# A decoder layer on one core: means and variances of the linear attention from rounded sums and their remainders, with roundings on ScalarE

## The chip, the core and the metric

The kernel runs on one core of a Trainium2 chip. The core has five engines that each work through their own instructions in order: TensorE (PE, with its weight loads as PEld), VectorE (DVE), ScalarE (ACT), GpSimd (POOL) and SyncE (SP, which only issues DMAs here). They wait for each other through semaphores. The metric is the device time of one execution in microseconds (us), the median of several.

## What is computed

A decoder layer over 8 batches of 512 tokens with 256 features. It has three parts, each followed by a layer norm. The first, linear attention within chunks of 32 tokens, is the one that the change is about:

```
Q, K, V = x @ W_q.T, x @ W_k.T, x @ W_v.T
S = (Qc @ Kc.T) * mask              # per chunk of 32 tokens, mask = decay ** (i - j) for i >= j
O = S @ Vc
out = sigmoid(x @ W_g.T) * O @ W_o.T + x
x = layernorm(x + out)
```

Then come a cross attention with 16 heads (`x = layernorm(x + xattn(x, ctx))`) and a feed-forward part with ternary weights and a low-rank term, of which only the weights concern us:

```
h = bitlinear(x, w_fc) + gate * (x @ v.T @ fast_b.T @ u.T)
out = bitlinear(relu(h) ** 2, w_proj)
```

## The kernel before

All activations are held with features on the 128 partitions (two halves, `DK` = 2) and the 512 tokens of a batch along the free dimension. The three parts are three phases. Each engine's program of a phase is one function (`_(pe)`, `_(dve)`, `_(act)`, `_(pool)`, `_(sp)`), written in the order in which it runs; nothing is reordered by a scheduler, and semaphores join the engines.

Where precision allows no plain rounding, an operand is split in two fp32r tiles, the rounded value (`_hi`) and the remainder (`_lo`), and three products hi·hi, lo·hi and hi·lo replace one fp32 product (`split_matmul`, L48 to L50). Plain fp32 products are kept for the scores (L57), attend (L747), the mean (L715), the variance (L719), and for some weight work.

The linear-attention phase goes through the batches in steps. Step b (1 to 7) works on batch b and finishes batch b - 1 and b - 2. In the order of each engine:

- TensorE (`step`, L770): `gates(b)` (12 products), `variance(b-2)`, `queries(b)` (12), `outputs(b-1)` (12), `scores(b)`, `values(b)` for tiles 0 and 1, `mean(b-1)`, `values(b)` for tiles 2 and 3, `attend(b)`. After step 2 comes `scale_means`, after steps 3 and 4 `low_rank`, whose result enters the feed-forward weights.
- VectorE (`step`, L631): `finish_y(b-1)` (two y_a, then tile_sum), `root(b-2)`, `mask_scores(b)`, `scale_x1(b-2)` (tile x_a), `split_x(b+1)` (x_hi, x_lo), `subtract_mean(b-1)` (dev_a), `gated(b)` (og_a), `sum_squares(b-1)`, `split_gated(b)` (og_hi, og_lo), and some weight work at the end.
- ScalarE (a loop at L480): `front(b)` (gate, with two table loads), `query_copies(b)` (qm), `deviation(b-2)` (three operations for the inverse root), `values(b)` (copies to v_tok), `square(b-1)` (sq_a).
- SyncE (`load_and_store`, L370): the load of x for batch b + 1 waits until y of batch b - 1 is finished (`y_out`), since it goes in the same half of `x_in`; behind it comes the store of x1.
- GpSimd splits the weights wq, wk and wv of the next phase (L405, L407), each after a load of 1 MB, and later works on the ternary weights (L414 to L423).

`tile_sum` holds first y's sum over the two halves, for the mean, and then the sum of the squares, for the variance. Both go through a product with `mean_w`, a 128x128 matrix of 1/256, into the PSUM bank `ST`.

The last batch's parts (`variance_late`, `outputs_last`, `mean_last`, `variance_last`) are issued by the cross-attention phase, among its first keys, queries and values. The cross attention and the feed-forward phase are not touched.

## Time and profile before

| | us |
|---|---|
| median of 3 runs | 1280.46 |
| lowest and highest | 1279.95, 1281.04 |
| the profiled execution | 1279.73 |
| its span, first to last instruction | 1277.7 |
| TensorE busy | 1256.6 (98%) |
| VectorE busy | 922.2 (72%) |
| ScalarE busy | 794.0 (62%) |
| GpSimd busy | 768.3 (60%) |

An engine's busy time is the time in which it has an instruction under way. Matmuls overlap in their pipeline, so a record is longer than what it takes from the stream; what a product costs is read from the distance of the starts. An fp32 product leaves two records, an fp32r product one. The chain of waits follows the end of the run back, at each step to what released it.

### The profile page before, as it was taken

What the parts mean: (1) busy time and instruction counts of PE and PEld (TensorE: products, weight loads), DVE (VectorE), ACT (ScalarE), POOL (GpSimd) and SP (SyncE); (2) the same over time, 40 slices, a digit from 0 to 9 for tenths busy, and PEclk for the clock granted to TensorE, in tenths of its full rate; (3) what the DMA queues carried; (4) which work ended last, traced back from release to release, by engine and by line L of the source; (5) the groups of instructions that cost most, each with busy time, mean ns of one, the idle gap of its engine ahead of it and who ended that gap; (6) DMA issues with size and microseconds to landing.
All of it is one profiled execution on the core that took longest, in us unless ns stands there. A gap on an engine that the chain in (4) does not pass through costs nothing.

```text
span 1277.7 us, 21198 instructions
## 1 busy us (share of the span) xinstructions
PE 1256.6 (98%) x6900; PEld 844.6 (66%) x6900; DVE 922.2 (72%) x1816; ACT 794.0 (62%) x1061; POOL 768.3 (60%) x445
## 2 busy tenths in 40 slices
PE   8999999999999999999999999999999999999996
PEld 6887856666666666656665666657566655677775
DVE  6888877656775767477577756784766777778887
ACT  3444457655665656566656655574656676788885
POOL 2532368967876679487768767794877687100000
PEclk9999999999999999999999999999999999999999
DMA  6311220001100110010011001100200110021101
GB/s 221 116 67 50 69 66 18 4 1 34 37 2 17 33 19 0 17 50 2 0 33 35 0 17 33 19 0 17 50 2 0 34 18 17 14 70 50 49 17 50
DMA packets 99391, 43.08 MB, mean 34 GB/s; under 512 B 77168, under 2 KB 82048, under 8 KB 99344
## 3 DMA queue, kind: packets, MB, share of 16 engines
q1 hardware_dynamic: 98528, 39.33, 12.4%
q0 software_dynamic: 816, 3.15, 0.7%
q8 instruction: 27, 0.44, 0.1%
q14 instruction: 20, 0.16, 0.0%
HBM read 29.59 MB, written 12.58 MB: 33 GB/s over the span
## 4 chain that ended last, share of the span: by engine, by line
PE 92%; DVE 3%; POOL 2%; issue 1%; ACT 1%; DMA 1%; SPq 0%; POOLq 0%; DVEq 0%
PE ps L1400 17%; PE ps L1375 15%; PE ps L48 12%; PE ps L50 11%; PE ps L49 11%; PE ps L1391 4%; PE ps L1379 4%; PE ps L1436 2%; PE ps L1435 2%; PE ps L1437 2%; PE ps L1412 2%; PE ps L1829 2%; PE ps L1830 2%; PE ps L747 1%; PE ps L57 1%
## 5 line engine op out<-in xcount | busy, mean ns | idle before, releaser
L1200 DVE CUSTOM_DVE_ANT_0 junk<-ps,mask 128x512 bf16<-128x512 f32 x504 | 315.0, 687 | 87.7 <-PE ps L1391 86.3
L1066 ACT ACTIVATE prob<-ps,mcol 128x1024 f32<-128x1024 f32 x256 | 282.2, 1117 | 128.9 <-PE ps L1379 124.0
L981 POOL TENSOR_TENSOR acc<-acc,prob 128x1024 f32<-128x1024 f32 x126 | 300.6, 2385 | 11.5 <-POOL acc L981 0.4
L978 POOL TENSOR_TENSOR acc<-prob 128x1024 f32<-128x1024 f32 x63 | 150.6, 2391 | 193.9 <-ACT prob L1066 192.9
L1400 PE MATMUL ps<-prob,v_b 128*64 128x512 f32 x1024 | 244.5, 598 | 0.0
L995 POOL TENSOR_TENSOR acc_lo<-acc,acc_hi 128x1024 f16<-128x1024 f32 x63 | 136.5, 2167 | 5.1
L1400 PEld LDWEIGHTS ps<-prob,v_b 128*64 128x64 f32 x1024 | 67.8, 136 | 107.4 <-issue 73.7
L1375 PE MATMUL ps<-q_hi,k_hi 64*128 64x512 f32 x512 | 114.3, 442 | 1.8 <-issue 0.7
L1379 PE MATMUL ps<-shift,ones_r 64*128 64x512 f32 x512 | 101.8, 392 | 0.1
L1375 PE MATMUL ps<-q_hi,k_lo 64*128 64x512 f32 x512 | 101.4, 391 | 0.0
L1375 PE MATMUL ps<-q_lo,k_hi 64*128 64x512 f32 x512 | 101.4, 390 | 0.0
L1391 PE MATMUL ps<-k_hi,q_hi 64*128 64x512 f32 x504 | 100.8, 394 | 0.0
L1211 DVE TENSOR_TENSOR ps<-ps,recip 128x512 f32<-128x512 f32 x64 | 44.7, 698 | 68.2 <-ACT recip L1081 68.2
L1073 ACT ACTIVATE pvc<-ps 128x512 f32<-128x512 f32 x64 | 38.4, 600 | 80.7 <-PE ps L1400 80.7
L1375 PEld LDWEIGHTS ps<-q_hi,k_hi 64*128 64x128 f32 x512 | 47.9, 183 | 53.6 <-ACT prob L1066 24.6
L1224 DVE SCALAR_TENSOR_TENSOR att_lo<-ps,bv,att_hi 128x512 fp32r<-128x512 f32 x64 | 48.1, 751 | 48.2 <-ACT att_hi L1089 48.2
L1234 DVE SCALAR_TENSOR_TENSOR q_lo<-ps,bq,q_hi 128x512 fp32r<-128x512 f32 x64 | 48.1, 752 | 31.1 <-ACT q_hi L1097 30.9
L1103 ACT ACTIVATE v_b<-ps 128x512 f32<-128x512 f32 x64 | 38.3, 598 | 50.2 <-PE ps L50 50.2
L1097 ACT ACTIVATE q_hi<-ps,bq 128x512 fp32r<-128x512 f32 x64 | 44.1, 690 | 35.7 <-PE ps L50 35.6
L991 POOL CAST acc_hi<-acc 128x1008 f16<-128x1008 f32 x63 | 64.4, 1022 | 0.0
L1089 ACT ACTIVATE att_hi<-ps,bv 128x512 fp32r<-128x512 f32 x64 | 44.1, 689 | 31.5 <-DVE ps L1219 31.5
L1079 ACT ACTIVATE recip<-ps 128x512 f32<-128x512 f32 x64 | 38.1, 596 | 34.6 <-PE ps L1412 34.6
(265 smaller groups left out, 2927.6 us busy)
## 6 DMA issues: line engine op xcount, KB each, us to landing
shift<-nmx SPq DMA_DIRECT2D x512, 0.5 KB, 2.0
x_in<-in_xT SPq DMA_DIRECT2D x8, 512.0 KB, 3.7
x_scratch<-x_a SPq DMA_DIRECT2D x8, 512.0 KB, 2.9
raw<-in_cT SPq DMA_DIRECT2D x8, 512.0 KB, 3.7
raw<-x_scratch SPq DMA_DIRECT2D x8, 512.0 KB, 3.9
y<-x_scratch SPq DMA_DIRECT2D x8, 512.0 KB, 3.7
y_scratch<-y SPq DMA_DIRECT2D x8, 512.0 KB, 2.8
outT<-x SPq DMA_DIRECT2D x7, 512.0 KB, 2.8
```

What stands on the lines that cost most here:

```text
L48: pe.matmul(out, lh, rh, start=(i == 0), stop=False)
L49: pe.matmul(out, lh, rl, start=False, stop=False)
L50: mm = pe.matmul(out, ll, rh, start=False, stop=(i == n - 1))
L978: pool.tensor_tensor(total, prob[:, 0], prob[:, 1], ALU.add).then_inc(acc_out, 1)
L981: pool.tensor_tensor(total, total, prob[:, kt], ALU.add).then_inc(acc_out, 1)
L995: pool.tensor_tensor(acc_lo[:], acc[:], acc_hi[:], ALU.subtract).then_inc(sum_lo_out, 1)
L1066: act.activation(prob[:, i].rearrange("p h t -> p (h t)"), SCORE[i % 2].rearrange("p h t -> p (h t)"), ACT.Exp, scale=SCALE, bias=mcol[:, ...
L1200: dve.tensor_tensor_reduce(junk[:, t % 2, h], SMAX[t % 2][:, h], mask[:], -1.0, -LOWEST, ALU.add, ALU.min, nmx[:, p % 2, t, h:h + 1]).then ...
L1375: pe.matmul(banks[:, h], l[OWN[h], par, cols], r[OWN[h], par], start=(n == 0), stop=False)
L1379: mm = pe.matmul(banks[:, h], ones_r[OWN[h], :], shift[OWN[h], par], start=False, stop=True)
L1391: mm = pe.matmul(SMAX[t % 2][:, h], q_hi[OWN[h], par, toks], k_hi[OWN[h], par], start=True, stop=True)
L1400: mm = pe.matmul(PV[OWN[h], :], v[:, kt, cols], prob[:, kt, h, :], start=(kt == 0), stop=(kt == NT - 1))
```

## The change

- Means and variances 0 to 6 are made from two tiles. ScalarE rounds tile_sum to `sum_hi`, VectorE subtracts to get `sum_lo`, and TensorE adds two fp32r products. Batch 7 keeps the fp32 product.
- The rounding of x (from batch 2) and of og_a (from batch 1) moves from VectorE to ScalarE; the remainders stay on VectorE. The low-rank scaling moves to ScalarE too. ScalarE's loop is written out.
- On TensorE `variance(b-2)` stands behind `queries(b)`, and all four tiles of values stand ahead of the mean.
- `sum_hi` and `sum_lo` share their memory with `sq_a`.
- The low-rank operands `uT` and `mid` are held twice, in partitions 0 to 15 and 64 to 79, and the two products of a call use one copy each. For that uT is loaded twice, and `middle` makes its product twice.

```diff
     dev = sb(ctx, "dev_a", [P, DK, T], F32)
-    sq = sb(ctx, "sq_a", [P, DK, T], F32)
+    with ExitStack() as squares:
+        sq = sb(squares, "sq_a", [P, DK, T], F32)
+    sum_hi, sum_lo = (sb(ctx, n, [P, T], F32R) for n in ("sum_hi_a", "sum_lo_a"))
...
+    RANK_ROWS = (slice(0, RANK), slice(DH, DH + RANK))
...
-        sp.dma_start(uT[:], a["uT"]).then_inc(f_in, 16)
+        for rows in RANK_ROWS:
+            sp.dma_start(uT[rows], a["uT"]).then_inc(f_in, 16)
...
+        def round_x(b):
+            act.wait_ge(x_in[b % 2], 8 * (b - b % 2) + 16)
+            act.wait_ge(qm_ps, 2 * b - 2)
+            act.activation(x_hi[:, b % 2], x[:, b % 2], ACT.Copy).then_inc(x_rounded, 1)
...
+        def mean_hi(b):
+            act.wait_ge(y_sum_out, b + 1)
+            if b > 0:
+                act.wait_ge(var_ps, b)
+            act.activation(sum_hi[:], tile_sum[:], ACT.Copy).then_inc(mean_hi_out, 1)
...
-        with act.Fori(2, B - 1, 2) as i:
-            for b in (i, i + 1):
-                front(b)
-                query_copies(b)
-                deviation(b - 2)
-                values(b)
-                square(b - 1)
+        for b in range(2, B):
+            front(b)
+            query_copies(b)
+            deviation(b - 2)
+            if b < B - 1:
+                round_x(b + 1)
+            mean_hi(b - 1)
+            values(b)
+            square(b - 1)
+            round_gated(b)
+            variance_hi(b - 1)
+            if b in (3, 4):
+                low_rank(b - 3)
...
+        def mean_lo(b):
+            dve.wait_ge(mean_hi_out, b + 1)
+            dve.tensor_tensor(sum_lo[:], tile_sum[:], f32(sum_hi[:]), ALU.subtract).then_inc(mean_lo_out, 1)
...
+        def sum_parts():
+            pe.matmul(ST, c["mean_r"][:], sum_hi[:], start=True, stop=False)
+            return pe.matmul(ST, c["mean_r"][:], sum_lo[:], start=False, stop=True)
...
         def step(b, par):
             gates(b, par)
+            queries(b, par)
             if b > 1:
                 variance(b - 2)
-            queries(b, par)
...
-            values(b, par, (0, 1))
-            if b == B - 1:
-                values(b, par, (2, 3))
+            values(b, par, (0, 1, 2, 3))
             if b == 1:
-                pe.wait_ge(f_mid, 1)
+                pe.wait_ge(f_mid, 2)
             mean(b - 1)
-            if b < B - 1:
-                values(b, par, (2, 3))
             attend(b)
```

On ScalarE, in the loop's step of batch b, before (inv_a and est_a are the inverse root of batch b - 2, v_tok the copies of the values):

```order
19 L445 ACTIVATE qm<-ps 128x512 [waits a_s_ps,a_qm_ps]
21 L445 ACTIVATE qm<-ps 128x512 [waits a_qm_ps]
24 L463 ACTIVATE inv_a<-ps,eps 128x512 [waits a_rs_out]
26 L465 ACTIVATE est_a<-inv_a 128x512 [waits a_est_out]
28 L467 ACTIVATE inv_a<-est_a 128x512 [waits a_est_out]
29 L456 ACTIVATE v_tok<-ps 128x512 [waits a_v_ps] x2
```

and after, in step 3 (x_hi is the rounded x of batch 4, sum_hi_a the rounded tile_sum, og_hi the rounded og_a):

```order
36 L474 ACTIVATE est_a<-inv_a 128x512 [waits a_est_out]
37 L476 ACTIVATE inv_a<-est_a 128x512 [waits a_est_out]
38 L481 ACTIVATE x_hi<-x_in 128x1024 [waits a_qm_ps,a_x_in_even]
39 L497 ACTIVATE sum_hi_a<-tile_sum_a 128x512 [waits a_var_ps,a_y_sum_out]
40 L465 ACTIVATE v_tok<-ps 128x512 [waits a_v_ps] x2
41 L460 ACTIVATE sq_a<-dev_a 128x1024 [waits a_sq_sum_out,a_dev_out]
42 L486 ACTIVATE og_hi<-og_a 128x1024 [waits a_y_ps,a_gate_used]
43 L501 ACTIVATE sum_hi_a<-tile_sum_a 128x512 [waits a_sq_sum_out]
```

The rounding of x, which waits for the load of x, stands ahead of the rounding of tile_sum, and og_hi ahead of the second one.

On VectorE, in step 3, before:

```order
72 L548 TENSOR_TENSOR tile_sum_a<-y_a 128x512 [waits a_var_ps,a_y_out]
73 L575 SCALAR_TENSOR_TENSOR rs_a<-ps,eps,inv_a 128x512 [waits a_x1_out,a_est_out]
74 L578 SCALAR_TENSOR_TENSOR rs_a<-rs_a,est_a 128x512 [waits a_rs_out]
75 L567 TENSOR_TENSOR s_masked<-ps,dmask 128x512 [waits a_o_ps,a_s_ps]
76 L585 SCALAR_TENSOR_TENSOR x_a<-dev_a,rs_a 128x1024 [waits a_stored,a_rs_out]
77 L501 CAST x_hi<-x_in 128x1024 [waits a_qm_ps,a_x_in_even]
78 L503 TENSOR_TENSOR x_lo<-x_in,x_hi 128x1024 [waits a_x_split]
```

and after:

```order
73 L594 TENSOR_TENSOR tile_sum_a<-y_a 128x512 [waits a_var_ps,a_y_out]
74 L629 SCALAR_TENSOR_TENSOR rs_a<-ps,eps,inv_a 128x512 [waits a_x1_out,a_est_out]
75 L632 SCALAR_TENSOR_TENSOR rs_a<-rs_a,est_a 128x512 [waits a_rs_out]
76 L603 TENSOR_TENSOR sum_lo_a<-tile_sum_a,sum_hi_a 128x512 [waits a_mean_hi_out]
77 L621 TENSOR_TENSOR s_masked<-ps,dmask 128x512 [waits a_o_ps,a_s_ps]
78 L639 SCALAR_TENSOR_TENSOR x_a<-dev_a,rs_a 128x1024 [waits a_stored,a_rs_out]
79 L548 TENSOR_TENSOR x_lo<-x_in,x_hi 128x1024 [waits a_x_rounded,a_x_in_even]
```

sum_lo_a, which waits for ScalarE, has come in ahead of the mask, x1 and x_lo, and the cast of x has gone.

## Rows read from the trace of the kernel before

**Rows 1.** The page's part on the chain that ended last, by line.

```profile
PE ps L1400 17%; PE ps L1375 15%; PE ps L48 12%; PE ps L50 11%; PE ps L49 11%; PE ps L1391 4%; PE ps L1379 4%; PE ps L1436 2%; PE ps L1435 2%; PE ps L1437 2%; PE ps L1412 2%; PE ps L1829 2%; PE ps L1830 2%; PE ps L747 1%; PE ps L57 1%
```

**Rows 2.** Busy time: length, PE, PEld, DVE, ACT, POOL, TensorE clock, DMA, GB/s.

```profile
57.00:75.50 18.50, 18.50 (x102) 14.76 (x101) 13.48 (x18) 9.06 (x12) 8.34 (x8) 1.00 0.19 66
```

**Rows 3.** Timeline of TensorE, step 6: start us, length us, engine, line, operation.

```profile
125.69 1.02 PE L715 MATMUL ps<-tile_sum_a,mean_w 128*128 128x512 f32 x2
...
127.97 2.01 PE L747 MATMUL ps<-s_masked,v_tok 128*128 128x128 f32 x16
129.74 0.47 PE L48 MATMUL ps<-x_hi,WgT_l_hi 128*128 128x512 f32 x1
...
132.56 1.02 PE L719 MATMUL ps<-tile_sum_a,mean_w 128*128 128x512 f32 x2
...
133.65 0.39 PE L49 MATMUL ps<-x_lo,M_l_hi 128*128 128x512 f32 x1
...
138.45 0.39 PE L49 MATMUL ps<-og_lo,WoT_l_hi 128*128 128x512 f32 x1
138.68 0.39 PE L50 MATMUL ps<-og_hi,WoT_l_lo 128*128 128x512 f32 x1
```

**Rows 4.** Timeline of VectorE, step 6.

```profile
122.67 0.69 DVE L543 SCALAR_TENSOR_TENSOR y_a<-x_in,ps 128x512 f32<-128x512 f32 x1 [0.67 <-PE ps L50]
123.39 0.69 DVE L548 TENSOR_TENSOR tile_sum_a<-y_a 128x512 f32<-128x512 f32 x1
...
125.39 0.68 DVE L567 TENSOR_TENSOR s_masked<-ps,dmask 128x512 f32<-128x512 f32 x1
125.99 1.22 DVE L585 SCALAR_TENSOR_TENSOR x_a<-dev_a,rs_a 128x1024 f32<-128x1024 f32 x1
127.12 0.69 DVE L501 CAST x_hi<-x_in 128x1024 fp32r<-128x1024 f32 x1
127.84 1.23 DVE L503 TENSOR_TENSOR x_lo<-x_in,x_hi 128x1024 fp32r<-128x1024 f32 x1
...
139.11 0.69 DVE L543 SCALAR_TENSOR_TENSOR y_a<-x_in,ps 128x512 f32<-128x512 f32 x1 [0.67 <-PE ps L50]
```

**Rows 5.** Timeline of VectorE, step 1, and the tile x_in's summary: issue to landing.

```profile
35.09 0.69 DVE L501 CAST x_hi<-x_in 128x1024 fp32r<-128x1024 f32 x1 [1.77 <-DMA x_in<-in_xT]
...
DMA to landing us min/median/max: 3.5/3.7/8.6
```

**Rows 6.** Timeline of ScalarE, step 6.

```profile
128.17 0.60 ACT L456 ACTIVATE v_tok<-ps 128x512 f32<-128x512 f32 x1 [1.69 <-PE ps L50]
130.23 1.06 ACT L451 ACTIVATE sq_a<-dev_a 128x1024 f32<-128x1024 f32 x1 [1.46 <-DVE dev_a L561]
```

**Rows 7.** Timeline of TensorE: scale_means after step 2, low-rank product after step 3.

```profile
54.53 1.88 PE L800 MATMUL ps<-scale,mean_w 128*128 128x512 f32 x4
...
57.04 0.48 PE L48 MATMUL ps<-x_hi,WgT_l_hi 128*128 128x512 f32 x1
...
73.66 1.98 PE L810 MATMUL ps<-uT,mid 16*128 16x512 f32 x4
...
75.57 0.50 PE L48 MATMUL ps<-x_hi,WgT_l_hi 128*128 128x512 f32 x1
```

**Rows 8.** Timeline of VectorE and GpSimd, step 5.

```profile
103.51 0.69 DVE L543 SCALAR_TENSOR_TENSOR y_a<-x_in,ps 128x512 f32<-128x512 f32 x1 [0.67 <-PE ps L50]
103.72 2.38 POOL L416 TENSOR_TENSOR wfc_raw<-wfc_raw,scale 128x1024 f32<-128x1024 f32 x1
104.23 2.42 DVE L548 TENSOR_TENSOR tile_sum_a<-y_a 128x512 f32<-128x512 f32 x1
```

**Rows 9.** Timeline of TensorE and VectorE, after step 7: variance(6) and og_lo of batch 7.

```profile
148.97 1.02 PE L719 MATMUL ps<-tile_sum_a,mean_w 128*128 128x512 f32 x2
...
149.39 1.23 DVE L600 TENSOR_TENSOR og_lo<-og_a,og_hi 128x1024 fp32r<-128x1024 f32 x1
```

**Rows 10.** The DMA issues of the first 170 us: engine, KB, median us to landing.

```profile
raw<-in_Wv POOLq DMA_DIRECT2D x1, 1024.0 KB, 8.9
```

More of the change, by code:

```diff
@@ L471, in _ @@
         values(0)
[L472 removed]
+        act.wait_ge(f_in, 112)
         act.activation(wabs[:], wfc[:], ACT.Abs).then_inc(f_abs, 1)
@@ L498, in split_x @@
             dve.wait_ge(x_in[par], 8 * (b - par) + 16)
-            if not (isinstance(b, int) and b < 2):
-                dve.wait_ge(qm_ps, 2 * b - 2)
-            dve.tensor_copy(x_hi[:, par], x[:, par]).then_inc(x_split, 1)
-            dve.wait_ge(x_split, 2 * b + 1)
-            dve.tensor_tensor(x_lo[:, par], x[:, par], f32(x_hi[:, par]), ALU.subtract).then_inc(x_split, 1)
+            if b < 2:
+                dve.tensor_copy(x_hi[:, par], x[:, par]).then_inc(x_split, 1)
+                dve.wait_ge(x_split, 2 * b + 1)
+            else:
+                dve.wait_ge(x_rounded, b - 1)
+            dve.tensor_tensor(x_lo[:, par], x[:, par], f32(x_hi[:, par]), ALU.subtract).then_inc(
+                x_split, 1 if b < 2 else 2)
         def split_weight(i, w, src):
@@ L553, in sum_squares, with variance_lo @@
             dve.tensor_tensor(tile_sum[:], sq[:, 0], sq[:, 1], ALU.add).then_inc(sq_sum_out, 1)
+        def mean_lo(b):
+            dve.wait_ge(mean_hi_out, b + 1)
+            dve.tensor_tensor(sum_lo[:], tile_sum[:], f32(sum_hi[:]), ALU.subtract).then_inc(mean_lo_out, 1)
+        def variance_lo(b):
+            dve.wait_ge(var_hi_out, b + 1)
+            dve.tensor_tensor(sum_lo[:], tile_sum[:], f32(sum_hi[:]), ALU.subtract).then_inc(var_lo_out, 1)
         def subtract_mean(b):
@@ L634, in step @@
                 root(b - 2)
+            mean_lo(b - 1)
             mask_scores(b)
@@ L643, in step @@
             split_gated(b)
+            variance_lo(b - 1)
             if b == 1:
@@ L667, in _ @@
         dve.wait_ge(f_mid_ps, 1)
-        dve.tensor_copy(mid[:], ST[0:RANK, 0:D]).then_inc(f_mid, 1)
+        for rows in RANK_ROWS:
+            dve.tensor_copy(mid[rows], ST[rows, 0:D]).then_inc(f_mid, 1)
         for b in range(1, B):
@@ L709, in gates @@
             mm.then_inc(g_ps, 1)
+        def sum_parts():
+            pe.matmul(ST, c["mean_r"][:], sum_hi[:], start=True, stop=False)
+            return pe.matmul(ST, c["mean_r"][:], sum_lo[:], start=False, stop=True)
         def mean(b):
[L712 to L713 removed]
+            if b > 0:
                 pe.wait_ge(rs_out, 2 * b - 1)
[L715 to L719 removed]
+            if b < B - 1:
+                pe.wait_ge(mean_lo_out, b + 1)
+                sum_parts().then_inc(mean_ps, 1)
+            else:
+                pe.wait_ge(y_sum_out, b + 1)
+                pe.matmul(ST, c["mean_w"][:], tile_sum[:], start=True, stop=True).then_inc(mean_ps, 1)
+        def variance(b):
+            if b < B - 1:
+                pe.wait_ge(var_lo_out, b + 1)
+                sum_parts().then_inc(var_ps, 1)
+            else:
+                pe.wait_ge(sq_sum_out, b + 1)
+                pe.matmul(ST, c["mean_w"][:], tile_sum[:], start=True, stop=True).then_inc(var_ps, 1)
         def values(b, par, tiles):
```

60 lines of the change are left out of this document (36 added, 24 removed).

## The prediction

> **What bounds the kernel now.** I read the chain of waits first. Nearly all of its time is TensorE (PE) time, and the attention lines L1400 and L1375, with the projections at L48 to L50, carry it [rows 1]. The change touches only the linear-attention phase, about the first 150 us. So the next view is the busy time of one stretch there: between 57.0 and 75.5 us TensorE is busy for 18.50 of 18.50 us at a granted clock of 1.00, while VectorE and ScalarE have slack [rows 2]. TensorE work removed there would be time gained, but only if TensorE still never waits. The third view is therefore one step (one batch, b = 6) in order of time on TensorE and VectorE [rows 3, 4]. The second y_a (L543) starts at 122.67, the last product of the next outputs starts at 138.68, and its y_a follows 0.43 us later, at 139.11. The step takes 139.11 - 122.67 = 16.44 us. I call the start of the second y_a zero. The mean starts at 3.02, the attend products (L747) at 5.30, and the next gates at 7.07.
>
> **What the change takes from TensorE.** A mean or variance is one fp32 product, and between its start and that of the second product behind it lie 133.65 - 132.56 = 1.09 us. A rounded 128x512 product takes 138.68 - 138.45 = 0.23 us of the stream, so the fp32 one takes 1.09 - 0.23 = 0.86, and the two rounded ones 0.46 [rows 3]. That is 0.40 us less, 14 times (means and variances 0 to 6): 5.6 us.
>
> The low-rank product takes 75.57 - 73.66 = 1.91 us now, as four records of two fp32 products [rows 7]. In two row groups one can run beside the other. Row groups do overlap here: the 1,536 records of L1375 take 15% of the span, or 0.125 us each, about half of the 0.23 us of a rounded product that is alone [rows 1, 3]. But each fp32 product is two records in a row, A A B B, and if a record waits only for the one ahead in its own group, only the second of A lies beside the first of B. A quarter goes: 1.91 to about 1.45, or 0.9 us over both calls. The ends are 0 and half of 1.91, twice. The Trainium skill, in "TensorE: Matmul & The Clock Gate", section Part 3 on packing small matmuls, gives the span of packed products as that of one product and some nanoseconds for each further one. By it each call would come to about 0.96 us, and the time below would be 1.0 us lower; no row here has such a pair alone. `middle` is doubled, and a second small load stands ahead of gate's load: +0.3 us, between 0 and 1.5.
>
> **Where the new waits stand.** The mean now needs, after tile_sum, a rounding on ScalarE (mean_hi) and a subtraction on VectorE (mean_lo). ScalarE works in order, and ahead of mean_hi(b-1) stands round_x(b+1). That waits for the load of x(b+1), which SyncE issues only when y(b-1) is out, in this very step. The order of instructions on ScalarE shows the pair. Before, x_hi was a cast on VectorE behind the mask and x1, where the load had landed. The load lands 3.5 us after its issue at best, 3.7 in the median; in the first step VectorE stood 1.77 us for it [rows 5]. Now, from zero:
> - y_a ends and the load is issued at 0.75 [rows 4]; it lands at 4.25 [rows 5].
> - round_x takes 1.06, the time of the square of the same shape [rows 6], to 5.31. mean_hi takes 0.60, that of a 128x512 copy [rows 6], to 5.91.
> - mean_lo starts at 5.94. By tile_sum and the mask (0.69 long; the next in line starts about 0.60 later) [rows 4] it ends at 6.63, and the mask starts at 6.55 and ends at 7.23.
> - The mean on TensorE would be due when all values are done. Their second half lies behind the mean now, so it is due at 127.97 - 0.86 - 122.67 = 4.44 [rows 3, 4]. It starts at 6.65: a wait of 2.2 us.
> - attend waits for the mask, starts at 7.25 and takes 129.74 - 127.97 = 1.77: 9.02.
> - On VectorE x1 takes 1.13 [rows 4], so x_lo starts at 8.28 and ends at 9.51. The next gates want it and start at 9.54, not at 7.07.
> - Gates to the next second y_a is 139.11 - 129.74 = 9.37 now [rows 3, 4], less 0.40 for the variance: 8.97.
>
> A plain step becomes 9.54 + 8.97 = 18.5 us; successive instructions on an engine overlap by some 0.1, so 18.4: **+2.0 us in a step** that was meant to lose 0.8. VectorE gets rid of two casts and the low-rank scaling, but that gives nothing, since it then waits for ScalarE. ScalarE's own load does not decide: it is busy for 9.06 us in the stretch of one step [rows 2], and two roundings of 1.06 and two of 0.60 bring it to 12.4 of 18.4. If qm is late by some tenths, that goes into the 2.2 us that the mean waits anyway. The remainder for the variance is made behind og_lo, about 5 us after x_lo; the variance, now behind the queries, comes 5.5 us after the gates start (12 gate and 12 query products at 0.23), so it just fits.
>
> **The sum.**
> - Step 1 has no x1, so attend's 9.02 decides: 17.99 against 16.44, +1.5.
> - Step 2 has scale_means behind attend, 57.04 - 54.53 = 2.51 us [rows 7]. TensorE is late by attend alone there, +1.5.
> - Steps 3 and 4 have the low-rank product behind attend. TensorE comes to the gates at 9.02 + 1.45 = 10.5 and x_lo is no longer late: 19.4 against 16.44 + 1.91 = 18.4, +1.0 each, +2.0 in all.
> - Step 5 lasts 122.67 - 103.51 = 19.16 now, 2.7 over a plain one, because tile_sum (2.42 instead of 0.69) and the operation after the root are drawn out while GpSimd works on wfc [rows 8, 4]. This falls into the new wait, whose end is set by the load and ScalarE: +2.0 - 2.7 = -0.7.
> - Step 6 is plain: +2.0.
> - Step 7 rounds no x. Its mean is later by mean_lo and earlier by nothing: +0.2.
> - Behind it, variance(6) is issued at 148.97, right after the first keys [rows 9]. Its remainder now stands on VectorE behind og_lo, which starts about when it does now, at 149.39, and frees the engine 1.14 later, and then takes 0.69. TensorE stands some 1.8 us (1.5 to 2.2) and saves 0.4: +1.4.
> - `middle` +0.3. And x(3) is loaded beside Wv, a 1,024 KB load that itself takes 8.9 us [rows 10]. The later x leaves, the more of it shares with Wv. Between 0 and 5.4 (8.9 - 3.5): I take 1.0, nearer to the undisturbed row, since x is half the size.
>
> Together 1.5 + 1.5 + 2.0 - 0.7 + 2.0 + 0.2 + 1.4 + 0.3 + 1.0 = 9.2 us. Everything after the phase starts later by this and runs as before, since it is TensorE's and none of it is changed. The profiled execution took 1279.73 us (its span of 1277.7 and 2.0 around it): 1288.9. The median of the runs lies 0.7 above it: 1289.6.
>
> **The rivals.**
> - *The load is no obstacle* (0.06). If the rounded x were there before mean_hi, TensorE would keep its pace: -5.6 - 0.9 + 0.3 + 1.4, so 1275.7. For it speaks that TensorE waits for VectorE almost nowhere now; against it the 3.5 us, which no load undercuts [rows 5]. It would need a landing 2.2 us earlier. This is the case on the other side, and at the same time the one in which the change does what it says.
> - *Half of it* (0.09). The first and last steps lose, but the rounding is quicker than a square and the contention that goes is worth more than 2.7 us: about +4, 1284.5.
> - *More than the sum* (0.20). sum_lo and tile_sum read and write only SBUF, as do the two operations that GpSimd draws out [rows 8]. In steps 1 and 2 GpSimd splits wk and wv. If a remainder is drawn out by 1.7 in three steps and the x load beside Wv takes 2 us more, it is +14, 1294.5.
> - *The clock falls* (0.01). The granted clock is 1.00 now [rows 2]. With gaps of 2.2 us in each step the upper level (2.4 GHz) might go. At 1.2 GHz a step's TensorE work, 16.44 - 0.80 = 15.6 us, would take 31.2, some 13 us more than 18.4, and over six steps about 78: 1367. The Trainium skill, in "TensorE: Matmul & The Clock Gate", in its part on the clock gate, says that the array falls back to the lower level when it idles; by that rule this rival needs gaps long enough, and the rows show none of this length inside the phase to tell.
>
> **How the numbers follow.** The forecast has 0.64: 1289.6, with its own range from 1286 to 1293, since the landing (3.5 or 3.7 in six steps, 1.2 us), the low-rank ends (1 us either way), `middle` and the remainder behind og_lo each move it by 1 to 2. To hold eight cases in ten the range takes in the half-way case and most of the upper one: 1284 to 1295. A measurement of this kernel tells about 0.2%, or 2.6 us, from no change. Faster has 0.06, within the bound 0.04 (the lower part of the half-way case), slower 0.90.
>
> **What would show it.** In the profile after, TensorE waits for VectorE at the mean, six times about 2.2 us, with VectorE's sum_lo as releaser, and VectorE waits for ScalarE's sum_hi; ScalarE waits for the DMA of x_in ahead of x_hi. Gates wait for x_lo by about 0.4 in steps 5 and 6. The second y_a's stand 18.4 apart in plain steps and 19.4 in those with the low-rank product. One variance waits 1.8 us behind the first keys. The records of the mean are 0.23 apart, and the low-rank product takes 1.45. If the load's wait stands in ScalarE but TensorE waits less than 1 us for a mean, the loop is wrong; if plain steps are 15.6 long, all of it is.

## The result

The changed kernel takes 1302.4 us (median of 4 runs, 1299.1 to 1303.6), the kernel before in the same series 1280.5: a ratio of 1.016 (95% interval 1.0145 to 1.0176), or 22 us more. The direction was as predicted, and so was the way in which the loss begins. The size was not: I had said 1289.6 and at most 1295. The profiled execution took 1303.59 us, with a span of 1301.8.

### The profile after

The whole loss lies in the linear-attention phase. From the last second y_a of the phase to the end of the span, the kernel before takes 1277.7 - 154.15 = 1123.6 us and the kernel after 1301.8 - 178.34 = 1123.5. So everything below is about the first 180 us.

TensorE's waits for other engines there (engine, what it wanted, who released it, line: us in total, times, longest), of the kernel after, 0 to 210 us:

```profile
PE ps L763 <- DVE sum_lo_a L603: 16.1, 7, 4.0
...
PE ps L763 <- DVE sum_lo_a L607: 3.8, 2, 3.4
PE ps L853 <- DMA gt<-in_gate: 1.2, 1, 1.2
```

L763 is the first of the two rounded products, for means and variances alike; L603 is the remainder for the mean, L607 that for the variance. The prediction put six waits of 2.2 us there. The trace has seven, 16.1 us in total: 2.23, 4.00, 1.80, 2.21, 2.27 and 2.08 in steps 1 to 6, and 1.54 in step 7, where the prediction had none. Step 6 in detail, TensorE, then VectorE, then ScalarE (start us, length us; in brackets the idle time before it and who ended it):

```profile
144.05 0.47 PE L763 MATMUL ps<-sum_hi_a,mean_w 128*128 128x512 f32 x1 [2.08 <-DVE sum_lo_a L603]
144.36 0.40 PE L764 MATMUL ps<-sum_lo_a,mean_w 128*128 128x512 f32 x1
144.59 3.36 PE L810 MATMUL ps<-s_masked,v_tok 128*128 128x128 f32 x16
147.60 0.77 PE L48 MATMUL ps<-x_hi,WgT_l_hi 128*128 128x512 f32 x1
```
```profile
137.35 0.69 DVE L589 SCALAR_TENSOR_TENSOR y_a<-x_in,ps 128x512 f32<-128x512 f32 x1 [0.67 <-PE ps L50]
...
143.21 0.69 DVE L603 TENSOR_TENSOR sum_lo_a<-tile_sum_a,sum_hi_a 128x512 fp32r<-128x512 f32 x1 [3.06 <-ACT sum_hi_a L497]
...
145.56 1.22 DVE L548 TENSOR_TENSOR x_lo<-x_in,x_hi 128x1024 fp32r<-128x1024 f32 x1
...
156.94 0.69 DVE L589 SCALAR_TENSOR_TENSOR y_a<-x_in,ps 128x512 f32<-128x512 f32 x1 [0.67 <-PE ps L50]
```
```profile
141.60 1.06 ACT L481 ACTIVATE x_hi<-x_in 128x1024 fp32r<-128x1024 f32 x1 [3.43 <-DMA x_in<-in_xT]
142.57 0.61 ACT L497 ACTIVATE sum_hi_a<-tile_sum_a 128x512 fp32r<-128x512 f32 x1
```

These answer to [rows 3, 4, 6]. ScalarE stands 3.43 us for the load of x, with the rounding of the mean's sum queued behind it; VectorE stands 3.06 us for that rounding; TensorE stands 2.08 us for the remainder. Counted from the second y_a (137.35), the mean starts at 6.70 (predicted 6.65) and x_lo at 8.21 (predicted 8.28). Up to there the step is the predicted one.

Then comes what was not predicted. attend (L810) takes 147.60 - 144.59 = 3.0 us, not 1.77, and the gates start at 10.25, not 9.54. The granted clock tells why (length, then busy us with instructions of PE, PEld, DVE, ACT, POOL, then TensorE's clock, DMA share, GB/s):

```profile
36.90:39.10 2.20, 0.04 (x1) 0.00 (x0) 0.77 (x2) 2.20 (x4) 0.00 (x0) 1.00 0.79 268
39.60:43.10 3.50, 3.50 (x19) 3.31 (x19) 2.28 (x3) 1.06 (x1) 1.64 (x2) 0.57 0.11 47
57.00:61.00 4.00, 0.24 (x3) 0.04 (x1) 1.43 (x1) 2.55 (x4) 3.84 (x5) 0.84 0.06 24
61.00:66.70 5.70, 5.46 (x20) 4.79 (x21) 5.70 (x6) 0.50 (x1) 5.54 (x4) 0.52 0.24 92
82.00:84.00 2.00, 0.20 (x3) 0.04 (x1) 0.85 (x2) 2.00 (x4) 0.00 (x0) 1.00 0.02 4
84.00:87.50 3.50, 3.50 (x22) 2.42 (x22) 3.50 (x4) 0.09 (x1) 0.00 (x0) 1.00 0.28 108
...
144.00:145.00 1.00, 0.95 (x6) 0.74 (x6) 1.00 (x2) 0.15 (x1) 0.00 (x0) 1.00 0.00 0
145.00:148.50 3.50, 3.50 (x17) 3.40 (x16) 3.41 (x4) 0.56 (x1) 0.00 (x0) 0.51 0.55 170
148.50:152.00 3.50, 3.50 (x17) 2.87 (x16) 2.90 (x4) 3.23 (x4) 0.00 (x0) 1.00 0.81 281
```

The first six rows are three pairs, each a gap of TensorE and the stretch behind it (steps 1, 2 and 3); the last three follow step 6. The clock is at half, the lower of its two levels (1.2 instead of 2.4 GHz), for about 3.5 us behind the gap, in step 2 for about 7, and then back. Behind the short gaps it falls only after TensorE has resumed, so the gap's own row looks harmless (1.00); in the 4 us of step 2 it falls within the gap. This happens in steps 1, 2, 4, 5 and 6 and behind the last variance, not in step 3, whose gap is 1.8 us. The stretch that was full at 1.00 before [rows 2] reads now:

```profile
57.00:75.50 18.50, 14.51 (x61) 11.66 (x60) 11.76 (x12) 10.30 (x13) 9.54 (x8) 0.82 0.09 33
```

The low-rank product of step 3, at the full clock, is the answer to [rows 7]:

```profile
83.99 0.47 PE L763 MATMUL ps<-sum_hi_a,mean_w 128*128 128x512 f32 x1 [1.80 <-DVE sum_lo_a L603]
...
84.53 2.02 PE L810 MATMUL ps<-s_masked,v_tok 128*128 128x128 f32 x16
86.48 1.13 PE L871 MATMUL ps<-uT,mid 16*128 16x512 f32 x4
87.54 0.50 PE L48 MATMUL ps<-x_hi,WgT_l_hi 128*128 128x512 f32 x1
```

It takes 87.54 - 86.48 = 1.06 us where it took 1.91.

### Where the 22 us are, step by step

The distance from the start of one second y_a to the next, in us (where two y_a stand in one row, x2, the second starts 0.69 before its end). The first starts at 30.85 before and at 32.32 after. "Predicted" is the distance before plus the prediction's term. "Again" is a second profiled execution of the kernel after, from the first of the experiments below (1302.2 us); e8, e12 and e5 are further experiments, labelled in their headings.

| step | before | predicted | after | again | e8 | e12 | e5 |
|---|---|---|---|---|---|---|---|
| 1 | 16.8 | 18.3 | 21.1 | 23.4 | 22.5 | 18.1 | 15.9 |
| 2 | 18.8 | 20.3 | 24.2 | 20.7 | 21.2 | 21.9 | 18.1 |
| 3 | 18.6 | 19.6 | 19.0 | 19.4 | 19.4 | 19.4 | 16.9 |
| 4 | 18.6 | 19.6 | 21.1 | 19.4 | 19.3 | 19.3 | 18.5 |
| 5 | 19.2 | 18.5 | 19.7 | 19.8 | 18.9 | 19.1 | 18.5 |
| 6 | 16.4 | 18.4 | 19.6 | 19.7 | 18.6 | 18.5 | 15.6 |
| 7 and last variance | 15.0 | 16.6 | 21.4 | 21.2 | 18.2 | 18.2 | 18.2 |
| from the first to the last | 123.3 | 131.2 | 146.0 | 143.4 | 138.0 | 134.6 | 121.7 |

The two executions of the same kernel differ step by step. In the second, steps 2, 3 and 4 take 20.7, 19.4 and 19.4 us, all within 0.4 of the prediction: TensorE waits there as long as elsewhere (2.18, 2.26 and 2.05 us), and the clock stays. Step 2's gap and the stretch behind it:

```profile
61.80:63.90 2.10, 0.00 (x0) 0.00 (x0) 0.80 (x2) 2.10 (x4) 0.48 (x1) 1.00 0.00 0
63.90:67.90 4.00, 3.96 (x22) 2.95 (x23) 4.00 (x5) 0.22 (x2) 0.00 (x0) 1.00 0.34 131
```

It falls in steps 1, 5 and 6, behind the last variance, and once ahead of the first y_a. Step 1 is the longest there because x(2) came late (5.6 us from issue to x_hi, against 3.7 in the first execution). So which gaps are followed by a fall changes from one execution to the next, and what it costs cannot be read from one trace alone.

### The profile page after: what moved, and what is told of

Read it like the earlier page. It is cut to its first block, busy times and chain, and to the rows that moved or that the text cites. A ratio compares the mean times of both kernels' runs of the same rounds, so it can differ in the third digit from the quotient of the medians.

```text
span 1301.8 us, 21211 instructions
## 1 busy us (share of the span) xinstructions
PE 1261.5 (97%) x6902; PEld 853.1 (66%) x6902; DVE 926.4 (71%) x1816; ACT 813.9 (63%) x1089; POOL 769.3 (59%) x445
## 4 chain that ended last, share of the span: by engine, by line
PE 88%; DVE 4%; DMA 3%; issue 2%; POOL 2%; ACT 1%; SPq 1%; DVEq 0%; POOLq 0%; ACTq 0%
PE ps L1462 17%; PE ps L1437 15%; PE ps L48 11%; PE ps L50 10%; PE ps L49 10%; PE ps L1453 4%; PE ps L1441 4%; PE ps L1497 2%; PE ps L1498 2%; PE ps L1499 2%; PE ps L1474 2%; PE ps L1891 2%; PE ps L1892 2%; DMA x_in<-in_xT 2%; PE ps L810 1%
## 5 line engine op out<-in xcount | busy, mean ns | idle before, releaser
L1296 DVE SCALAR_TENSOR_TENSOR q_lo<-ps,bq,q_hi 128x512 fp32r<-128x512 f32 x64 | 48.1, 751 | 33.3 <-ACT q_hi L1159 32.8
```

## The experiments

Each kernel was timed beside the kernel before on the same chip (1280.0 to 1281.0 in each of the series).

### The kernel after, once more (the table's column "again")

> The changed kernel once more, on the chip of the next three, so that they can be compared with it: 1298 to 1304 us, granted clock of the span 0.988 to 0.992.

Measured: 1301.0 us (1299.7 to 1304.2), ratio 1.0155 (1.0135 to 1.0175). The kernel before has 1281.0 in this series, so the loss is 20.0 us; in the first series it was 21.9. This run is on one chip with e5, e6 and e7. The other experiments ran on other chips, and are compared by their distance to the kernel before of their own series.

### A third buffer for x (e5)

```diff
-            sp.wait_ge(y_out, 2 * b - 2)
-            sp.dma_start(x[:, par], batch_cols(a["xT"], b)).then_inc(x_in[par], 16)
+            if b > 2:
+                sp.wait_ge(y_out, 2 * b - 4)
...
+            sp.dma_start(X[b % 3], batch_cols(a["xT"], b)).then_inc(x_in[b % 3], 16)
```

> The changed kernel in its own order on every engine, but x has three buffers (the third shares its memory with the constant bits), so that the load of x(b+1) is issued a step earlier and has landed when ScalarE comes to round it. Theory W (the load's wait ahead of mean_hi is the start of the whole loss): ScalarE no longer stands for the load, the mean waits under 0.5 us in plain steps, clock 1.00 but for one stretch at the last variance, plain steps 15.6 to 16.0 us, 1276 to 1283 us. Theory G (two more roundings in ScalarE's order and GpSimd's hold on VectorE): steps above 17 us, above 1290 us.

Measured: 1280.8 us (1279.4 to 1283.5), ratio 1.0001 (0.9992 to 1.0011). The order of all engines is that of the kernel after; only the load leaves a step earlier. In step 6 ScalarE and VectorE then do what the change wanted:

```profile
121.68 1.04 ACT L486 ACTIVATE x_hi<-x_in 128x1024 fp32r<-128x1024 f32 x1
122.62 0.62 ACT L502 ACTIVATE sum_hi_a<-tile_sum_a 128x512 fp32r<-128x512 f32 x1
```
```profile
120.29 0.69 DVE L594 SCALAR_TENSOR_TENSOR y_a<-x_third,ps 128x512 f32<-128x512 f32 x1 [0.67 <-PE ps L50]
...
123.28 0.69 DVE L608 TENSOR_TENSOR sum_lo_a<-tile_sum_a,sum_hi_a 128x512 fp32r<-128x512 f32 x1
...
135.87 0.69 DVE L594 SCALAR_TENSOR_TENSOR y_a<-x_in,ps 128x512 f32<-128x512 f32 x1 [0.68 <-PE ps L50]
```

No bracket stands behind x_hi: the load has landed. The step from 120.29 to 135.87 takes 15.6 us, the 16.44 of before less two times 0.40, as priced. So the wait for the load, with all that follows from it, is the whole loss of this series: 20.2 us between this kernel and the one after, 20.0 between before and after. This is the main result, and it is shown by adding a buffer, not by taking a wait away.

### The rounding of x behind the rounding of the sum (e1)

```diff
+            mean_hi(b - 1)
             if b < B - 1:
                 round_x(b + 1)
-            mean_hi(b - 1)
```

> The changed kernel with one thing moved: on ScalarE the rounding of x stands behind mean_hi instead of ahead of it. Theory W (the loss starts with the wait for the x load in front of mean_hi, and the low clock follows from TensorE's gaps): no gap over 1 us at the mean, granted clock 1.00 through the linear attention, 1276 to 1282 us. Theory G (the loss comes from roundings on ScalarE and from GpSimd drawing out the new VectorE operations, wherever x is rounded): the mean still waits, still low-clock stretches, above 1292 us.

Measured: 1290.0 us (1287.6 to 1292.3), ratio 1.0083 (1.0062 to 1.0103). The loss is 10.1 us in its own series. About half of it is gone, less than expected (1276 to 1282), since the wait has a new place. Nor did the clock stay up: in the profiled execution it falls in step 5, behind a gap of 1.94 us, and behind the last variance. The value copies stand behind round_x now, and attend needs them:

```profile
PE ps L763 <- DVE sum_lo_a L603: 4.9, 4, 1.9
...
PE ps L810 <- ACT v_tok L465: 3.8, 4, 1.2
PE ps L763 <- DVE sum_lo_a L607: 3.4, 1, 3.4
```

Whatever is put behind a waiting instruction of ScalarE inherits its wait. I had moved one victim out and left the other.

### Both repairs of the order, and two small ones (e7)

```diff
+            mean_hi(b - 1)
+            values(b)
             if b < B - 1:
                 round_x(b + 1)
-            mean_hi(b - 1)
-            values(b)
```

The second uT load also goes behind the first loads, on a semaphore of its own, and variance 6 is one fp32 product again.

> Two buffers for x, its rounding on ScalarE behind mean_hi and the value copies, and the two repairs. x_lo comes at 7.3 us after y at the earliest (3.5 landing, 1.06 rounding, 1.23 remainder and the copies), so that plain steps are 16.2 to 16.6 us, as before; the low-rank product gains 1.7: 1277 to 1282 us. Rival: with every rounding behind the load the square and og_hi are late too, over 1285.

Measured: 1284.4 us (1282.3 to 1287.1), ratio 1.0025 (1.0014 to 1.0035). That is between the two expectations. The order, with two buffers and with what the two small repairs bring, regains 16.6 of the 20 us. x_lo is late now (1.7 us over three waits), since x is rounded last, and TensorE still waits 5.1 us for the mean's remainder, over three waits in steps 4, 5 and 7.

### x rounded on VectorE again (e3)

```diff
-                dve.wait_ge(x_rounded, b - 1)
+                dve.tensor_copy(x_hi[:, par], x[:, par]).then_inc(x_split, 1)
```

> The changed kernel with the rounding of x back on VectorE, as before; all else as changed. Theory W: ScalarE no longer waits for the load, the mean waits under 1 us, clock 1.00, 1276 to 1282 us. Theory G: above 1292 us. It differs from moving the rounding on ScalarE by 0.6 us more on VectorE in each step, which should cost at most 2 us in all.

Measured: 1283.2 us (1282.3 to 1287.8), ratio 1.003 (1.0014 to 1.0045). All else of the change is kept. No load stands in ScalarE's queue, and the loss against before is 3.3 us where the kernel after has 20.0 or 21.9. The mean still waits up to 1.94 us, where under 1 was expected. In the profiled execution (1283.15, at the median) the clock falls behind that gap, in step 4, for about 7 us, and that step takes 22.5 us instead of the 18.6 of before; that is as much as the whole remaining loss.

### Means and variances as fp32 products (e4)

```diff
-                pe.wait_ge(mean_lo_out, b + 1)
-                sum_parts().then_inc(mean_ps, 1)
+                pe.wait_ge(y_sum_out, b + 1)
+                pe.matmul(ST, c["mean_w"][:], tile_sum[:], start=True, stop=True).then_inc(mean_ps, 1)
```

> The changed kernel with all means and variances as one fp32 product of tile_sum again (no sum_hi, no sum_lo); the roundings of x and og_a stay on ScalarE, x ahead of the value copies. Theory W: the mean waits for nothing on ScalarE, so the load wait in ScalarE costs only what the value copies behind it delay attend (their end moves to about 6.3 us after y, 1 us late): 1281 to 1287 us with the fp32 products' 5.6 us back. Theory G (the roundings on ScalarE as such): above 1290 us.

Measured: 1283.1 us (1280.0 to 1288.0), ratio 1.0025 (1.0013 to 1.0038), as expected. round_x still waits for its load in ScalarE, but no sum stands behind it any more. The value copies do:

```profile
75.75 1.06 ACT L481 ACTIVATE x_hi<-x_in 128x1024 fp32r<-128x1024 f32 x1 [5.18 <-DMA x_in<-in_xT]
76.71 1.07 ACT L465 ACTIVATE v_tok<-ps 128x512 f32<-128x512 f32 x2
```
```profile
77.44 2.02 PE L798 MATMUL ps<-s_masked,v_tok 128*128 128x128 f32 x16 [0.64 <-ACT v_tok L465]
```

ScalarE stands 5.18 us here and TensorE pays 0.64 (4.8 us over six such waits in all, the longest 2.19 in step 2): a copy is one operation long, while the split sum is a chain of rounding, remainder, product, mask. Together with the experiment before, this says that the rounding of x on ScalarE and the split sums, each without the other, leave a loss of about 3 us; the other 17 to 19 are their meeting in one queue.

### Dummy products that hold the clock (e2 and e8)

```diff
+            if b < B - 2:
+                fill(16 if b == 1 else 9, QO[:, 0])
             if b > 0:
                 pe.wait_ge(rs_out, 2 * b - 1)
```

Two kernels add work: the first issues 8 dummy products (14 in step 2) just ahead of the wait for the remainder, the second 9 (16) ahead of every wait of the mean; both put 10 ahead of variance 6. The diff is of the second.

> The changed kernel with TensorE kept at work in its new gaps: ahead of each of the waits for sum_lo of the means 0 to 5, 8 rounded 128x512 products (14 for the mean 1) of 0.23 us into the bank that the mean overwrites anyway, and 10 ahead of variance 6. They add work and take no wait away. Theory C (the half clock after the gaps costs about 11 us, and the waits themselves the rest, about 9): clock 1.00 through the phase, 1290 to 1294 us. Rival N (the low clock falls in times in which TensorE is early anyway and costs nothing): clock 1.00, and still 1299 to 1304 us. If the fill runs past the end of the wait, at most 2 us more.

> The kernel after with dummy products that keep TensorE busy in its waits, now issued ahead of every wait of the mean (nine rounded 128x512 products into the bank of queries that is free there, 16 in the second step) and ten ahead of variance 6. Nothing is left out; work is added. It settles how much of the loss is the granted clock. Theory C (the fall of the clock costs 1.2 to 1.7 us behind each gap of 2 us and more): the clock shows 1.00 from 20 to 180 us, attend takes 1.8 us in every step, the last second y_a of the phase starts at or before 171 us instead of 177 to 178, and the time is 1290 to 1297. Theory N (the waits are the loss, the clock only goes with them): the clock shows 1.00 too, but the last second y_a stays at 175 us or later, and the time is 1299 to 1304.

Measured: 1298.2 us (1297.5 to 1299.4), ratio 1.0146 (1.0129 to 1.0163), and 1296.6 us (1295.4 to 1297.5), ratio 1.0127 (1.011 to 1.0144). Every stretch of 20 us between 20 and 180 us shows a granted clock of 1.00 in both; the kernel after shows 0.98, 0.93, 0.84, 1.00, 0.91, 0.91, 0.91, 0.91. The waits are filled, not removed. The first lies between its two expectations: it loses 18.3 us to before where the kernel after loses 20.0 or 21.9, and its interval overlaps with that of the kernel after. The second loses 15.6, which is 4 to 6 us less, as its theory C had it; all its executions (1295.4 to 1297.5) lie below all eight of the kernel after (1299.1 to 1304.2). So that much at least of the loss is the clock. The step table says more: with the clock held, steps 3 to 6 of e8 take 19.4, 19.3, 18.9 and 18.6, together 76.1 where the prediction has 76.0.

It is not the length of the gap alone that decides, as the second execution of the kernel after has already shown. In step 1 of e8 TensorE stands longest, and the clock stays:

```profile
36.00:39.30 3.30, 3.30 (x20) 2.59 (x18) 0.00 (x0) 0.00 (x0) 0.00 (x0) 1.00 0.97 390
39.30:42.30 3.00, 0.04 (x1) 0.00 (x0) 0.81 (x2) 2.41 (x4) 2.46 (x3) 1.00 0.00 1
42.30:46.00 3.70, 3.69 (x24) 3.17 (x25) 3.70 (x4) 0.98 (x2) 3.54 (x4) 1.00 0.00 0
```

What else it depends on is not settled by these runs.

### The dummies, and GpSimd's splitting cut short (e12)

```diff
-                part = (slice(None), j // 2, slice(j % 2 * T, j % 2 * T + T))
+                part = (slice(None), j // 2, slice(j % 2 * T, j % 2 * T + (16 if i else T)))
```

> The kernel after with the dummy products that hold the clock, and with GpSimd's split of Wk and Wv on 16 of 512 columns in each chunk (the rest is set to zero at the start), so it leaves out the weights that the later phase would need. Steps 1 and 2 took 22.6 and 21.1 us with the dummy products alone, where I had predicted 18.4 and 20.2. Theory P (VectorE drawn out by GpSimd makes the difference): no VectorE operation of the sums and remainders in steps 1 and 2 is above 1.3 us, step 1 takes 20 us or less, step 2 20.5 or less, and the time is 2.5 to 4 us below the 1296.6 of the dummy products alone. Theory Q (the line of work on VectorE and ScalarE itself is too long there, the late load of x(2) above all): step 1 stays above 21.5 and the time within 1.5 us.

Measured: 1291.9 us (1291.3 to 1292.5), ratio 1.0085 (1.007 to 1.01), 4.6 below e8, slightly more than expected. Step 1 falls from 22.5 to 18.1, where 18.3 was predicted. The end of step 1 on VectorE, first in the kernel after, then here:

```profile
45.74 1.63 DVE L655 TENSOR_TENSOR og_lo<-og_a,og_hi 128x1024 fp32r<-128x1024 f32 x1
47.29 1.78 DVE L607 TENSOR_TENSOR sum_lo_a<-tile_sum_a,sum_hi_a 128x512 fp32r<-128x512 f32 x1
48.99 3.88 DVE L707 TENSOR_REDUCE psc<-wfc 128x256 f32<-128x2048 f32 x1
52.79 1.27 DVE L589 SCALAR_TENSOR_TENSOR y_a<-x_in,ps 128x512 f32<-128x512 f32 x2
```
```profile
44.62 1.23 DVE L660 TENSOR_TENSOR og_lo<-og_a,og_hi 128x1024 fp32r<-128x1024 f32 x1 [0.52 <-ACT og_hi L491]
45.76 0.69 DVE L612 TENSOR_TENSOR sum_lo_a<-tile_sum_a,sum_hi_a 128x512 fp32r<-128x512 f32 x1
46.36 3.88 DVE L712 TENSOR_REDUCE psc<-wfc 128x256 f32<-128x2048 f32 x1
50.17 1.37 DVE L594 SCALAR_TENSOR_TENSOR y_a<-x_in,ps 128x512 f32<-128x512 f32 x2
```

The two y_a start back to back: step 1 ends on VectorE, which is late by its line of work, not on TensorE. In such a step each drawn-out operation counts in full (sum_lo 1.78 instead of 0.69). From the mean's sum_lo to the first y_a VectorE takes 54.54 - 41.49 = 13.05 us in e8 and 50.17 - 38.73 = 11.44 in e12, so the contention is 1.6 us of the 4.4. The rest is the load: ScalarE's x_hi waits for x(2) until 39.89 in e8 and until 37.11 in e12. In e8 GpSimd issued Wk's 1 MB load at 32.86, ahead of SyncE's issue of x(2) at 33.34; in e12 (33.92 and 33.45) and in the kernel after (33.66 and 33.03) it came behind. A large load ahead of it cost x(2) 2.9 us (6.55 from issue to x_hi, against 3.66), in that execution. The kernel after is not spared this: in its second profiled execution Wk was issued at 33.36 and x(2) at 34.47, and x_hi started 5.56 us later. Step 2 does not fall (21.9), contrary to what was expected: the 16 dummies there end at 59.05, 1.4 us after the remainder is ready at 57.61, so without them it would be 20.5, and 20.3 was predicted.

### GpSimd's work on the ternary weights cut short (e9)

All three of GpSimd's operations on wfc are cut in this way; one is shown.

```diff
-            pool.tensor_tensor(wfc[:, k], wfc[:, k], scale[:], ALU.mult).then_inc(f_step, 1)
+            pool.tensor_tensor(wfc[:, k, 0:16], wfc[:, k, 0:16], scale[:, 0:16], ALU.mult).then_inc(f_step, 1)
```

> The kernel after, with GpSimd's three operations on wfc on 16 of 1,024 columns, so it leaves out most of that part of the ternary weights. It asks what the drawn-out VectorE operations of steps 4 and 5 are worth. Theory P (GpSimd's work on the same SBUF port draws VectorE out and this stands on the path): in steps 4 and 5 no VectorE operation of the mean is above 1.3 us, each of those two steps is 1 to 2 us shorter, and the time is 1298.5 to 1301. Theory W (the waits for the load hide it, as my prediction had it for step 5): the VectorE operations shorten but the steps 4 and 5 stay within 0.5 us of those of the kernel after, and the time is 1301.5 to 1304.

Measured: 1303.7 us (1296.9 to 1305.4), ratio 1.0188 (1.0171 to 1.0205). The drawn-out operations are gone in steps 4 and 5, and ScalarE's rounding is waited for as before:

```profile
97.21 0.69 DVE L632 SCALAR_TENSOR_TENSOR rs_a<-rs_a,est_a 128x512 f32<-128x512 f32 x1
100.65 0.69 DVE L603 TENSOR_TENSOR sum_lo_a<-tile_sum_a,sum_hi_a 128x512 fp32r<-128x512 f32 x1 [2.75 <-ACT sum_hi_a L497]
```

The steps speak for the prediction's view that these operations hide in the wait for the load. Steps 4 and 5 take 19.3 and 19.6 us here, and 19.4 and 19.8 in the second execution of the kernel after, which like this one has no fall of the clock in step 4 and one in step 5; the mean's sum_lo starts 5.9 and 6.0 us after the second y_a of step 4. The profiled execution is the fastest of the five, 6.9 us under the median, so the median itself, which is no lower than that of the kernel after, is not explained by a trace: the clock over the whole span is 0.992 in that execution and 0.987 to 0.988 in the other four.

### What the pieces are worth when no load is in the way

Three kernels: three buffers, with the second uT load moved and variance 6 as fp32 (e6); the same with all sums as fp32 products (e10); and the kernel before with the low-rank product in two row groups and nothing else (e11), whose diff is shown. The first two were timed once more on e11's chip.

```diff
+    RANK_ROWS = (slice(0, RANK), slice(DH, DH + RANK))
-                mm = pe.matmul(VY[:, n], mid[:, k * P:(k + 1) * P], uT[:, n * T:(n + 1) * T], start=True, stop=True)
+                mm = pe.matmul(VY[:, n], mid[RANK_ROWS[n], k * P:(k + 1) * P], uT[RANK_ROWS[n], n * T:(n + 1) * T],
+                               start=True, stop=True)
```

> Three buffers for x, and two repairs: the second load of uT behind all other first loads, on a semaphore of its own, and the variance 6 as one fp32 product, so that it needs no remainder behind og_lo. If the start (1.2 us of TensorE waiting for the gate's load) and the last variance (3.4 us, with the low clock behind it) are lost as the trace of the changed kernel shows, it is 3 to 6 us below the three buffers alone: 1272 to 1278 us, below the kernel before. If it is equal to them, the time there was hidden.

> The version with three buffers of x and the second uT load behind all others, but every mean and variance as one fp32 product again. Nothing is left out. It asks whether the split sums pay at all once no load stands in their way. Theory S (each split sum saves the 0.40 us that the rows of before gave, 13 of them left in the best version so far, and one fp32 sum waits less for its rounding): 5 us slower than the best version so far (1279.4), so 1283 to 1286. Theory H (ScalarE's and VectorE's extra operations take back what TensorE saves): within 1.5 us of it, 1278 to 1281.

> The version with three buffers of x and both repairs, once more, on the same chip as the low-rank product alone and as its twin with fp32 sums. Split sums worth what TensorE's rows say (theory S): 5 us faster than the twin. Worth nothing (theory H, which the first runs of the two on different chips spoke for: 1279.4 and 1279.2): within 1 us of it and within 1 us of the low-rank product alone.

> The twin with fp32 sums, once more, on the same chip. Theory H: within 1 us of the version with split sums, and within 1 us of the low-rank product alone, since x rounded on ScalarE takes nothing from TensorE. Theory S: 5 us slower than the version with split sums.

> The kernel before with one part of the change alone: the low-rank product in two row groups, with the second uT load behind all first loads on a semaphore of its own. Nothing is left out. Theory L (the low-rank product is all that the change has to give): the four records take 1.06 us instead of 1.91, the step with compare_in and the one behind it are 0.85 us shorter each, middle costs nothing, and the time is 1278.8 to 1279.8 where the kernel before has 1281.0. Rival (the start is later by the doubled middle and copy, and VectorE or GpSimd take the rest): 1280.5 to 1281.5.

| | us | ratio to before |
|---|---|---|
| e6, split sums | 1279.4, again 1279.6 | 0.9984 (0.9975 to 0.9993), 0.9983 (0.9974 to 0.9992) |
| e10, fp32 sums | 1279.2, again 1280.2 | 0.9987 (0.9978 to 0.9997), 0.9991 (0.9982 to 1.0000) |
| e11, low rank alone | 1281.8 | 1.0007 (0.9998 to 1.0016) |

The version with three buffers and split sums beats both kernels, the one before by 1.4 to 1.6 us, at the edge of what can be told. Expected were 1272 to 1278: the two small repairs bring 1.4 us (1280.8 to 1279.4), not 3 to 6. In the time of the runs split sums make no difference that can be told (0.2 us against them, then 0.6 for them). In the profiled phases, from the first second y_a to the last, they make 1 us: 120.3 and 120.5 in e6, 121.4 and 121.5 in e10. Thirteen sums by 0.40 would be 5.2. The steps show where the rest goes. In both profiles of e6 steps 4 and 5 take 37.0 us together, in those of e10 35.3, so the split loses 1.7 us just there, while steps 3 and 6 are 0.8 shorter each with it. In steps 4 and 5 GpSimd draws VectorE out, a split sum is two operations longer on the way to TensorE than an fp32 one, and TensorE waits for the remainder by up to 2.0 us.

The low-rank product alone saves what it should on its own row and nothing at the end, where 1.2 to 2.2 us less than before were expected. It takes 1.06 us, and step 3 lasts 17.7 us instead of 18.6; step 4 stays at 18.5. Then, in step 5, TensorE meets VectorE, which GpSimd draws out there as it did before. Before, these were tile_sum and the root's second operation [rows 8]; here they are the latter (2.10) and x1. TensorE waits long enough for the clock to fall (VectorE, TensorE, then the stretches around the gap):

```profile
109.27 2.79 DVE L588 SCALAR_TENSOR_TENSOR x_a<-dev_a,rs_a 128x1024 f32<-128x1024 f32 x1
```
```profile
113.98 0.50 PE L48 MATMUL ps<-x_hi,WgT_l_hi 128*128 128x512 f32 x1 [2.31 <-DVE x_lo L506]
```
```profile
111.70:114.00 2.30, 0.02 (x1) 0.02 (x1) 2.27 (x4) 0.00 (x0) 0.00 (x0) 1.00 0.43 166
114.00:115.50 1.50, 1.50 (x7) 1.24 (x8) 1.50 (x2) 0.41 (x1) 0.00 (x0) 1.00 0.25 96
115.50:118.50 3.00, 3.00 (x8) 2.26 (x7) 2.97 (x4) 2.20 (x3) 0.00 (x0) 0.50 0.00 0
```

Step 5 takes 20.6 instead of 19.2: the saving is handed back, and the clock with it. That this is so in every execution of it is not shown; one was profiled.

## Why the prediction was right, and where it was wrong

Right:

- **The place of the wait.** ScalarE's x_hi waits for the load, the sum's rounding behind it, VectorE for that, TensorE for the remainder: all four rows stand in the trace, and a third buffer takes the loss away.
- **Its size.** Six waits of 2.2 predicted, 16.1 us over seven measured; the mean at 6.70 after y_a, 6.65 predicted; plain step 18.5 and 18.6 with the clock held, 18.4 predicted.
- **Step 5's term**, that the drawn-out operations fall into the wait: 18.9 with the clock held, 18.5 predicted; cutting GpSimd's work left steps 4 and 5 as long as they are in the second execution of the kernel after.
- **The split sum's saving on TensorE**, 0.40 each: e5's plain step is 15.6.

Wrong, in the order of size:

- **The rival on the clock** got a chance of 0.01 and the wrong shape, and the sum had no term for it. This is the step of the prediction that failed first. I priced the fall as all or nothing, a whole step at 1.2 GHz, found 1367 us absurd, and dropped it. The traces show a part: some 3.5 us at half speed behind a gap, sometimes 7. Half of that, 1.7 us or 3.5, is lost of TensorE's work, and of a plain fall the steps pay 0.8 to 1.8 us. By the step table, after against e8, the clock is 3.0 + 1.8 + 0.8 + 1.0 + 3.2 = 9.8 us in steps 2 and 4 to 7 of the first execution, and again against e8 it is 0.9 + 1.1 + 3.0 = 5.0 us in steps 5 to 7 of the second. The medians, by the distance to before, give 4 to 6, and that with e8's dummies overrunning and its x(2) late. The rows for pricing it were there: a plain step with 15.6 us of TensorE work and a gap of the predicted length, and a fall of any length behind it costs at most half its time. The Trainium skill, "TensorE: Matmul & The Clock Gate", Part 1, describes such a pattern, one fall with each wait of a loop, but for waits of about 3 to 5 us; here waits of 2.1 to 2.3 us did it in some executions, and waits as long did not in others. Its price, half of the throttled time, fits the rows: 3.5 us at 0.51.
- **Step 1 and step 2** (1.5 each). I let attend decide, as in a plain step. In step 1 VectorE decides, which reduces wfc for 3.9 us at the end of it, so everything that delays VectorE behind the mean's remainder counts. From that remainder to the next y_a are 52.79 - 38.33 = 14.46 us in the kernel after, 13.05 in e8 and 11.44 in e12. The first difference, 1.4, is the clock: og_a stands 1.42 us for attend, which runs at half, and in e8 it stands for nothing. The second, 1.6, is what GpSimd draws out. I had this mechanism as a rival with 0.20, three times 1.7 us; it holds in step 1. In step 2 of the kernel after two remainders are drawn out as well (the mean's to 1.52 us, x's to 2.28), and how much of that step's 3.0 us over e8 they hold is open. The 1.0 us for x(3) beside Wv was not seen (it was there 3.9 us after its issue, near the ordinary landing). x(2) behind Wk was not in the sum, and cost 1.9 us in the second execution and 2.9 in e8.
- **The last step** (+0.2 and +1.4). 18.2 us with the clock held against 16.6. The variance waits 3.42 us in the kernel after, and making it fp32 again takes 18.2 to 16.3 in e6 against e5, so its split costs 1.9. The other 1.3 is step 7's mean: it rounds no x, but GpSimd draws out its remainder (2.88 instead of 0.69 in e6) and TensorE waits 1.30.
- **The start** (+0.3): 32.32 and 33.76 in the two executions against 30.85. `middle` waits 1.16 and 1.50 us there, for gate's load behind the second uT load. That this wait costs as much is not shown: with that load moved (e6, e10, e11) the first second y_a starts at 31.3 to 32.8 as well. It moves between executions for other reasons (x_hi's wait between 0.5 and 1.8).
- **The low-rank product**, 1.45 predicted, 1.06 measured. The rule for packed products in the Trainium skill gave 0.96 and was the nearer one; my reading that the second record of each pair must wait for the one ahead did not hold. Step 3 shows little of it: 19.0 in one execution of the kernel after and 19.4 in the other, where the loop gave 19.4.

Together, from the first second y_a to the last, the first execution is 146.0 - 131.2 = 14.8 us over the prediction. By the above the clock has about 11 of it (9.8 and 1.4), GpSimd's hold on VectorE in step 1 has 1.6, and the last step without the clock has 1.6.

The range failed for the same reason as the value: its upper end held the contention rival and nothing of the clock. That rival was also added up wrongly: 9.2 + 3 * 1.7 + 2 is 16.3, not 14, so it stood at 1296.7 and not at 1294.5. Six falls of 1.7 us beside the sum would have given 1299.8.

## What to carry to other kernels

An instruction that waits for a DMA holds everything behind it on its engine. Before moving such an instruction to another engine, list what is queued behind it there, and who waits for that; if it must stay, a buffer more (here 20 us) or a place behind what others wait for (17 us, with the small repairs) pays. When an edit opens gaps of about 2 us in TensorE's stream, add to the upper end of the range half of a low-clock stretch behind each, since some of them will be followed by one and some not; and when an edit shortens TensorE's work by less than 1 us where a slower engine is close behind, as the low-rank product alone did, expect to find it again as a wait.
